# First attention layer of a graph network: one tile in seven gets its signs on VectorE, and two in seven get the lower half of their counts there

## The reference

```
h = x @ W
logits = leaky_relu(h[src] @ a_s + h[dst] @ a_d, 0.2)
m = segment_max(logits, dst)
e = exp(logits - m[dst])
denom = segment_sum(e, dst)
coef = e / (denom[dst] + 1e-16)
out = segment_sum(coef[:, None] * h[src], dst) + b
```

## Time and profile before

| | |
|---|---|
| three executions | 2966.0, 2967.22, 2977.09 us |
| profiled execution | 2972.84 us, span 2971.0 us |
| TensorE (PE) busy | 2569.7 us, 86% of the span |
| VectorE (DVE) busy | 2307.2 us, 78% |
| ScalarE (ACT) busy | 1604.4 us, 54% |
| mean granted TensorE clock | 0.934 |
| first attention layer, tiles | 1107.8 to 1447.7 us of the span |

### The profile page before, as it was taken

The page is one execution under the profiler, slowest core; times in us unless marked ns, Lnnn a source line. Parts: engine busy times, 40 slices in busy tenths (PEclk is TensorE's granted clock), DMA queues, the critical chain, the costliest instruction groups (busy, mean ns, idle before and its releaser), DMA issues. The chain is left out here.

```text
span 2971.0 us, 77270 instructions
## 1 busy us (share of the span) xinstructions
PE 2569.7 (86%) x26152; PEld 2159.6 (73%) x26153; DVE 2307.2 (78%) x5557; ACT 1604.4 (54%) x2016; POOL 355.0 (12%) x866
## 2 busy tenths in 40 slices
PE   3648999999999959999787888759999967999998
PEld 2645666666666649999666777649999957888997
DVE  8979999999999966676699999979999995222212
ACT  6023444444444349999797888658888841000101
POOL 0003344434444300000000000000000000000000
PEclk8878999999999979999999999879999978999999
DMA  3003443343344436667345545315545616888898
GB/s 102 0 1 83 119 121 82 100 134 88 94 118 110 134 109 218 231 224 256 134 153 174 193 157 191 130 66 175 195 161 186 215 65 241 306 301 300 314 368 297
DMA packets 448144, 493.83 MB, mean 166 GB/s; under 512 B 132101, under 2 KB 447465, under 8 KB 447850
## 3 DMA queue, kind: packets, MB, share of 16 engines
q1 hardware_dynamic: 300920, 409.16, 41.2%
q10 hardware_dynamic: 147060, 82.71, 9.5%
HBM read 402.61 MB, written 89.17 MB: 166 GB/s over the span
## 5 line engine op out<-in xcount | busy, mean ns | idle before, releaser
L2594 PE MATMUL psum<-sb_arena 128*128 128x198 bf16 (+2 forms) x14406 | 1118.1, 238 | 148.0 <-DVE sb_arena L1881 86.5
L2594 PEld LDWEIGHTS psum<-sb_arena 128*128 128x128 f16 x14406 | 1045.0, 99 | 220.8 <-DVE sb_arena L1881 139.6
L3211 ACT ACTIVATE sb_arena<-sb_arena 128x896 f16 (+1 forms) x1029 | 1016.4, 1046 | 157.6 <-PE psum L2594 122.2
L1875 DVE TENSOR_TENSOR sb_arena<-sb_arena 128x896 f16<-128x896 f16 x1029 | 634.9, 621 | 139.4 <-ACT sb_arena L3211 117.9
L1166 DVE TENSOR_SCALAR sb_arena<-sb_arena 128x392 f16<-128x392 f16 x2352 | 582.1, 312 | 0.0
L2873 ACT ACTIVATE sb_arena<-psum 128x784 f16<-128x784 f32 x392 | 323.3, 825 | 440.4 <-PE psum L2240 388.8
L2240 PE MATMUL psum<-sb_arena 128*128 128x392 f16 x2352 | 483.6, 343 | 39.7 <-ACT sb_arena L2835 22.2
L2659 PE MATMUL psum<-sb_arena 128*128 128x192 bf16 x4802 | 412.1, 247 | 27.2 <-DVEq L2006 15.7
L2659 PEld LDWEIGHTS psum<-sb_arena 128*128 128x128 f16 x4802 | 401.4, 98 | 36.7 <-DVEq L2006 16.4
L1881 DVE TENSOR_TENSOR sb_arena<-sb_arena 128x896 f16<-128x896 f16 x686 | 423.0, 617 | 0.0
L2240 PEld LDWEIGHTS psum<-sb_arena 128*128 128x128 bf16 x2352 | 290.6, 128 | 165.9 <-issue 63.8
(11 more groups left out here) (378 smaller groups left out, 1267.6 us busy)
## 6 DMA issues: line engine op xcount, KB each, us to landing
sb_arena<-counts SPq DMA_DIRECT2D x245, 896.0 KB, 6.6
sb_arena<-counts SPq DMA_DIRECT2D x245, 672.0 KB, 4.6
counts<-sb_arena ACTq DMA_DIRECT2D x56, 1344.0 KB, 5.6
sb_arena<-records SPq DMA_DIRECT2D x392, 6.0 KB, 1.7
sb_arena<-records ACTq DMA_DIRECT2D x392, 6.0 KB, 1.7
counts<-sb_arena SPq DMA_DIRECT2D x1, 5488.0 KB, 19.6
records<-sb_arena SPq DMA_DIRECT2D x1, 3124.0 KB, 8.9
counts<-sb_arena ACTq DMA_DIRECT2D x14, 112.0 KB, 1.7
```

The costliest lines, as they stand in the source:

```text
L1875: nc.vector.tensor_tensor(above_at[r % RING], above_at[r % RING], counts_of(g, j), ALU.mult).then_inc(above_ready, 1)
L2594: last = nc.tensor.matmul(psum[:, bank, at:at + wide], of[:, b * BLK:(b + 1) * BLK], moves[side][:, r, :], start=(r == 0 and at == 0), sto ...
L3211: nc.scalar.activation(above_at[r % RING], of, ACT.Sigmoid, bias=steep_s[:, r:r + 1], scale=STEEP).then_inc(signs_ready, 1)
```

## The change

In the first attention layer alone, by the tile's number modulo 7:
- tile 3 of each seven (`OWN_SIGN`): ScalarE makes no signs. VectorE makes `above` in one scalar_tensor_tensor: (target score row > minus source score) times counts. It waits itself until the tile seven back has been used. The minus source scores (`against`) are one small operation per layer.
- tiles 1 and 5 of each seven (`WITH_BELOW`): VectorE also makes `below`, counts minus `above`, behind the next tile's `above`. TensorE multiplies `above` by u alone (99 columns) and `below` by v (99 columns), in place of 198 and 99. The subtraction in `fold_pieces` stays right, since the tile adds its below part where the whole counts went, and nothing to what is taken off.
- the numbers that the semaphores wait for follow. In tiles 1 and 5 `tile_used` is counted up behind the tile's last matmul, in place of the first of its second half.

```diff
+OWN_SIGN = 3
+WITH_BELOW = (1, 5)
...
+                        if l == 0:
+                            nc.vector.tensor_scalar(against[:], scores[:, :, 0], -1.0, None, ALU.mult)
...
-                    dve.wait_ge(signs_ready, c * NB + (n * ROWS + r + 1))
-                    nc.vector.tensor_tensor(above_at[r % RING], above_at[r % RING], counts_of(g, j), ALU.mult).then_inc(above_ready, 1)
+                    if own_sign(l, r):
+                        of = ROW2[:, bass.ds(c * CW, CW)] if not isinstance(c, int) else ROW2[:, c * CW:(c + 1) * CW]
+                        if not (isinstance(c, int) and c == 0 and r < RING):
+                            dve.wait_ge(tile_used, c * NB + (n * ROWS + r + 1 - RING))
+                        nc.vector.scalar_tensor_tensor(above_at[r % RING], of, against[:, r:r + 1], counts_of(g, j), ALU.is_gt, ALU.mult).then_inc(above_ready, 1)
+                    else:
+                        dve.wait_ge(signs_ready, c * sign_tiles(l) + (signs_before(l) + sign_tiles(l, r + 1)))
+                        nc.vector.tensor_tensor(above_at[r % RING], above_at[r % RING], counts_of(g, j), ALU.mult).then_inc(above_ready, 1)
...
                         count_above(c, r)
-                        if l > 0 and r > 0:
+                        if r > 0 and with_below(l, r - 1):
                             count_below(c, r - 1)
-                        elif l > 0 and not first:
+                        elif r == 0 and l > 0 and not first:
                             count_below(c - 1, NB - 1)
...
-                        elif l > 0:
-                            pe.wait_ge(below_ready, c * NB + ((n - 1) * ROWS + r + 1))
+                        elif with_below(l, r):
+                            pe.wait_ge(below_ready, c * below_tiles(l) + (below_before(l) + below_tiles(l, r + 1)))
                             of = below_at[r % RING]
...
-                        wide = moves[side].shape[2]
+                        wide = wide3 if l == 0 and with_below(l, r) else moves[side].shape[2]
...
-                            if l == 0 and side == 1 and b == 0:
+                            if l == 0 and side == 1 and b == (CB - 1 if with_below(l, r) else 0):
                                 last.then_inc(tile_used, 1)
...
-                        signs(c, r)
+                        if not own_sign(l, r):
+                            signs(c, r)
```

More of the change, by code:

```diff
@@ L417, in gnn_kernel @@
         steep_s, tail = view(tail, [BLK, NB], fp32)
+        against, tail = view(tail, [BLK, NB], fp32)
         above, tail = view(tail, [BLK, NB], fp32)
@@ L468, in banks_before, with own_sign, with_below, sign_tiles @@
             return sum(len(parts[k][7]) * CHUNKS for k in parts if k < l)
+        def own_sign(l, r):
+            return l == 0 and r % GRP == OWN_SIGN
+        def with_below(l, r):
+            return l > 0 or r % GRP in WITH_BELOW
+        def sign_tiles(l, r=NB):
+            return sum(not own_sign(l, k) for k in range(r))
+        def signs_before(l):
+            return sum(CHUNKS * sign_tiles(k) for k in range(l))
+        def below_tiles(l, r=NB):
+            return sum(with_below(l, k) for k in range(r))
+        def below_before(l):
+            return sum(CHUNKS * below_tiles(k) for k in range(l))
         def groups_full(l):
@@ L1881, in count_below @@
                     nc.vector.tensor_tensor(below_at[r % RING], counts_of(g, j), above_at[r % RING], ALU.subtract).then_inc(below_ready, 1)
-                    if j == GRP - 1:
+                    if l > 0 and j == GRP - 1:
                         dve.drain().then_inc(cnt_free, 1)
@@ L2593, in tile @@
                             seen.add(k)
-                            last = nc.tensor.matmul(psum[:, bank, at:at + wide], of[:, b * BLK:(b + 1) * BLK], moves[side][:, r, :],
+                            last = nc.tensor.matmul(psum[:, bank, at:at + wide], of[:, b * BLK:(b + 1) * BLK], moves[side][:, r, 0:wide],
                                                     start=(r == 0 and at == 0), stop=(r == NB - 1), skip_group_check=True)
-                            if l == 0 and side == 1 and b == 0:
+                            if l == 0 and side == 1 and b == (CB - 1 if with_below(l, r) else 0):
                                 last.then_inc(tile_used, 1)
```

## The result

The changed kernel takes 2957.2 us (median of 13 executions, 2944.6 to 2966.6), the kernel before, run beside it, 2973.55 us (13 executions). The ratio is 0.9937, 95% interval 0.9922 to 0.9953: 19 us less (14 to 23), where 22.4 were forecast. The two medians lie 16.35 us apart. The profiled execution took 2954.33 us, its span is 2952.4.

A forecast was written before the change was run, and what follows sets the result against it. ScalarE bounded narrowly; after the change three engines at 41.2, 40.6 and 41.0 us a chunk, so their waits decide. -6.6 - 3.4 - 4 x 3.1 - 0.2 + 0.2 = -22.4 us: 2967.2 to 2945 us, 8-in-10 range 2934 to 2965.

The forecast's parts named there:

- Steps 1 and 2: Per chunk, ScalarE loses 7 signs (6.5 us) and needs 41.2 us; TensorE saves 4.1 us, 40.6 in place of 44.7.
- Step 3: VectorE per chunk: 14 added differences (7.5 us), seven own signs at 1.00 us pitch replacing products; it needs 41.0 us.
- Rival C: VectorE becomes the bound, own sign at half rate plus computed addresses, 2.14 us each: +10 us, 2977 us; chance 0.08.
- Step 4: Chunk boundary: TensorE's wait at tile 48 for ScalarE's copies becomes 1.0 us in place of 1.8; tile 0 keeps 0.5.
- Step 5: Tile 12: its difference stands behind the fold, TensorE waits 2.5 us (0.7 before); middle chunk 44.6 us, -3.1.
- Rivals A: The fold stays as well hidden as now (0.7 us), 1.8 us more gain in chunks 1 to 5: 2936 us; chance 0.14.
- B: Lock step after the fold: each new-kind tile waits some 0.35 us, chunks 1 to 5 gain nothing: 2962 us; chance 0.18.
- Step 6: Chunk 0 has no fold: TensorE takes up chunk 1 at 1153.4 in place of 1160.0, -6.6 us, the largest single gain.
- Step 7: Chunk 6: VectorE's hidden_early and added work make TensorE wait 7.4 us by tile 21; 48.9 us, -0.2.
- step 8: `against` adds 0.2 us; transfers cost nothing; clock stays at 1.00, and a fall in chunk 6 would coincide with VectorE waits.

The follow-up runs named there:

- fold_spread: Changed kernel with the fold in five steps behind tiles 13, 20, 27, 34, 41 (last chunk 8 to 12): ratio 0.9916 to the kernel before, layer 307.2 us.
- fold_late: Changed kernel with the first attention layer's fold behind tile 41 instead of 12, except in the last chunk: ratio 0.9929 to the kernel before, layer 314.9 us.
- fold_at_13: Changed kernel with the first attention layer's fold behind tile 13 instead of 12: layer 316.5 us, middle chunk 44.7 us.
- below_1_4: Changed kernel with lower halves in tiles 1 and 4 of each seven instead of 1 and 5: layer 318.9 us, middle chunk 44.9 us.
- evict5: Changed kernel with ScalarE's bank copies in the first attention layer one tile earlier: layer 323.9 us, middle chunk 45.2 us.
- below_only: Changed kernel without the own sign, only lower halves in tiles 1 and 5 of each seven: ratio 1.0019 to the kernel before, layer 345.8 us.
- spread_evict5: Changed kernel with the fold in five steps and ScalarE's bank copies one tile earlier: layer 308.6 us, middle chunk 43.1 us.

## Why the prediction was right, step by step

The mechanism held: three engines level at 41 to 42 us, and time decided by their waits.

- Steps 1 and 2 (ScalarE, TensorE). ScalarE is busy 41.95 us in a middle chunk (41.2 by pitches). TensorE's chunk without waits is 40.7 us (40.6).
- Step 3 (own sign). 1.145 us, pitch 1.06; forecast 1.09 and 1.00. The line through the two-source rows gave 1086 ns, and the instruction took 5% more than that the earlier trace rows. The Trainium skill's halving for two non-bf16 sources ("Vector Engine (DVE) Microarchitecture Reference", "Points that are easy to get wrong") did not show in this instruction, whose sources are fp32 and fp16: by the rates in rows 8 it would have been a pitch of 1.94 us. Rival C falls with it.
- Step 4 (boundary). 1.2 us, forecast 1.0. I had ScalarE's sign start 0.1 us into tile 48; it started 0.3 us into it (at 1281.38 - 0.94 = 1280.44; tile 48 began on TensorE at 1280.12). The last matmul of tile 47 is recorded until 1280.28, so about half of the delay is that matmul's end, and the other half passed before the sign began.
- Step 5 (fold). The wait is 2.56 us in the middle chunks, forecast 2.5, and tile 12 was reached at P + 10.60, forecast 10.6; the experiments with the fold show the cause. (The 0.7 us of the kernel before, which the prediction puts at tile 12, stood ahead of tile 13.) Rivals A (0.7 us) and B (a wait at each new tile) are out: the 409 matmuls behind it show no wait.
- Step 6 (chunk 0). 43.9 us, forecast 43.65, -6.3 us against 50.25.
- Step 7 (chunk 6). 49.15 us, forecast 48.9. TensorE starts tile 21 at P + 25.64, forecast 25.3. The clock fell once here too, for 3.4 us from P + 19.1, but it lies among waits for VectorE, whose work sets the time of these tiles, so little of it shows, as step 8 had said. In `fold_spread`, where it did not fall, this chunk took 48.8 us; the fold's steps stood elsewhere there, so the two are no exact pair.
- Step 8 (the clock) failed in one point: "waits of 2.5 us leave it at 1.00". In chunks 2 and 5 the clock fell to 0.50 for 3.4 us behind the fold's wait, 1 us after its end, at a cost of 1.6 us each, 3.2 together; in chunks 1, 3 and 4 the clock stayed at 1.00 behind waits of 2.2 to 2.6 us. The transfers came as forecast (250 GB/s, forecast 251). That the later layers only start earlier is not shown: the part behind the layer was 6.0 us longer in the profile.

The miss of the layer, 321.0 against 315.3 us, is 3.2 us of clock, 1.2 of boundary (six times 0.2), and 0.1 to 0.2 a chunk of small terms. So 4.4 of the 5.7 us lie in the waits and in the clock behind them; the small terms are not traced further. The whole execution came nearer to the forecast (19 us by the ratio) than the layer did (16.9 us); its interval of 14 to 23 us holds both figures, so that nearness may be chance.

## What to carry to other kernels

When engines run level, moving work is worth what the handovers leave: the lower halves alone took 4 us of work a chunk from TensorE, put 7.5 us on VectorE, and made the layer 8 us longer; only with the own sign did they pay. Before moving work onto an engine, look for the longest uninterrupted job in its queue and compare it with its lead over its consumer; cutting that job (4.0 us) into steps of under 1 us gave nearly as much in this layer (13.8 us, 3.2 of them clock) as the change itself (16.9), though whole executions do not yet show the difference clear of their noise. Moving one wait earlier, as with the copies, only helps when nothing behind it has used that slack already.

## What the runs showed of the hardware that was not expected

The granted clock fell for 3.4 us behind some waits of TensorE of 2.6 us and not behind others of the same length. Windows over the fold's wait and behind it, in chunk 2 and in chunk 3 of the changed kernel:

```profile
1201.00:1205.00 4.00, 1.59 (x30) 1.44 (x28) 3.39 (x9) 1.52 (x3) 0.00 (x0) 1.00 0.85 307
1205.00:1208.50 3.50, 3.50 (x38) 3.39 (x37) 3.50 (x7) 2.70 (x3) 0.00 (x0) 0.52 0.46 89
...
1247.00:1251.00 4.00, 1.63 (x30) 1.48 (x28) 3.34 (x8) 1.84 (x2) 0.00 (x0) 1.00 1.01 362
1251.00:1254.50 3.50, 3.50 (x62) 3.50 (x60) 3.50 (x7) 3.21 (x4) 0.00 (x0) 1.00 0.30 53
```

In those 3.5 us TensorE did 38 matmuls in the one case and 62 in the other. With waits of at most 1.9 us (`fold_late`, `fold_at_13`, `fold_spread`) no fall came in chunks 1 to 5. With 2.2 us (`below_1_4`) it came in one of five, with 3.5 us (`evict5`) in two of five, and with waits of some 4 us (`below_only`) at all six boundaries. A single long wait is not needed: in chunk 6 of `spread_evict5`, where several waits follow each other, a fall came behind two of 1.3 and 1.8 us. In the kernel before a wait of over 3 us passed without one. What decides between two equal waits stays open.
